# A decoder of six residual blocks on one core: golden gate weights split into four steps, constants moved, statistics between additions

## The chip, the core and the metric

One NeuronCore of a Trainium2 chip runs the whole program. TensorE (PE) multiplies matrices into eight PSUM banks of 128 x 512 floats, VectorE (DVE), ScalarE (ACT) and GpSimd (POOL) do the elementwise work, and SyncE (SP) issues most transfers. Each engine has its own list of instructions, carried out strictly in that order, and waits on semaphores for the others. The metric is the device time of one execution in microseconds (us), the median of several.

## The reference

The input x has 4 sequences of 256 tokens of 256 numbers, so 1024 tokens. Six blocks follow, each of the form "add, then normalize over the 256 numbers":

```
x = layernorm(x + linear_attention(x))            # 16 heads, elu + 1
x = layernorm(x + expert_by_token_id(x))          # 4 experts, one for each token
x = layernorm(x + golden_experts(x))              # 8 experts, all computed, weighted
x = layernorm(x + grouped_attention(x))           # groups of 32, 16 heads
x = layernorm(x + cross_attention(x, ctx, mask))
x = layernorm(x + top2_experts(x))                # 8 experts of 176, plus a shared one
```

The third is the one that the change is about. Every expert computes `(silu(x @ Wg) * (x @ Wu)) @ Wd`, and the eight results are added with weights that come from a small chain over 8 numbers per token:

```
inh      = sigmoid(x @ Wr / temperature)
in_zone  = (inh >= LOWER) & (inh <= UPPER)
distance = |inh - 1/e|
weights  = exp(-distance / 0.1) * in_zone
no_expert = sum(weights) < 1e-8
fb   = exp(-distance / 0.3), kept for the top 2 experts only, divided by its sum
weights  = fb where no_expert else weights
weights  = weights / max(sum(weights), 1e-8)
```

All results are float32. A float32 product is made of three products of rounded parts (high x high, high x low, low x high), so each operand is split into a rounded "high" part and the "low" rest.

## The kernel before, in words

The tokens are 8 tiles of 128. They are worked on in two halves, 4 tiles (512 tokens) each. Block 3, the golden experts, is done for the first half with the 8 experts and then for the second half again; it is software-pipelined with the blocks before and behind it. Its parts have these names in the program and below:

- Slot s (0 to 67) is one chunk of 128 hidden units of an expert, for 512 tokens. Expert unit u has slots 2u and 2u+1. Slots 8 to 23 are the golden experts for the first half, 24 to 39 for the second. Here m8 means step m of slot 8.
- **g** and **u** (TensorE): the gate and the up product of a slot, 6 matmuls each with 512 columns (L548, L549, L551), into banks 0 to 3. A gate product waits for the silu of the slot before the last, an up product for the hidden product (m) of two slots before.
- **s** (ScalarE L1233): silu of the gate. **m** (VectorE L1888): silu x up into `hraw`. **h** (ScalarE L1247): the high part of it. **l** (GpSimd L1489): the low part, `h_lo = hraw - h_hi`.
- **d** (TensorE L877 to L879): the down product of one expert unit, 24 matmuls of 256 columns, into banks 4 and 5, a pair of tiles in each. It waits for l of both slots of the unit, and, before it overwrites a bank, for the addition of the unit before.
- **a** (VectorE L1902): `x_tok += bank * weight`, 4 tiles, in two pairs. So a10 adds unit 10, and d11 can start only when the first pair of a10 is done.
- **G** and **D**: split of the weights of a unit into high (ScalarE L1265, L1276) and low (GpSimd L1495, L1500).
- **r0.n** and **r1.n**: the golden router for the first and the second half. r.3 is logits and sigmoid, r.4 the distance on VectorE (L1953, L1954) and its two exponentials on ScalarE (L1302, L1303), r.5 the whole chain of golden weights on VectorE (L1921 to L1940): two operations for the zone mask, three for the near weights, max and max_index for the top 2 with four behind them, and 13 more, nearly each waiting for the one before on a semaphore.
- **e0.10**, **e1.10** (VectorE L1626 to L1632): the statistics of the norm behind the golden block, for example 0 and 1 of the half (an example is one sequence of 256 tokens, two tiles); **e2.10**, **e3.10** for the second half. **c** (VectorE L1766 to L1770): constants for the later cross attention. **k4** (L1731 to L1735): which expert owns which block of the token-routed experts. **x1.50** to **x1.53** (L1761, L1763): additions and statistics for the second half of block 2.

The order of steps on each engine is written out by hand, in five lists of names (SP_ORDER, PE_ORDER, ACT_ORDER, POOL_ORDER, DVE_ORDER); the lists of PE, POOL and SP are the same before and after. The piece of PE's list that matters below is

```
g11 d4 u11 g12 u12 g13 u13 g14 u14 d5 g15 u15 d6 ...
g21 d9 u21 g22 u22 g23 u23 d10 d11 g24 u24 g25 u25 g26 e0.12 e1.12 u26 g27 u27 a0.3 d12 a0.4
```

Of the kernel before, what the change touches and what calls it, by code (L numbers as in the profile page):

```python
# [19 lines left out]
HT = TILES // 2  # L20
# [162 lines left out]
a4 m11 x1.51 m12 x1.52 x1.53 r1.0 m13 m14 a5 a6 m15 m16 m17 r1.2 a7 r1.3 a8 m18 r1.4 m19 m20 a9 m21 m22 m23 a10 a11
e0.10 e1.10 m24 r1.5 m25 e0.12 e1.12 m26 c a0.3 a12 a0.4 m27 a0.5 a0.6 m28 a0.7 m29 a0.8 a13 m30 a0.9 a0.10 a14 m31
a0.25 m32 m33 a0.11 e0.0 a15 a0.26 e1.0 m34 a16 e0.2 e1.2 m35 e0.3 e1.3 m36 e0.4 e1.4 m37 e0.5 e1.5 m38 a17 m39 e0.7
e1.7 a18 a0.22 a19 e2.10 e3.10 a0.23 m40 e2.12 e3.12 a1.3 a1.4 m41 m42 a1.5 a1.6 a1.7 a1.8 o43 m43 a1.9 o44 m44 a1.10
a1.25 o45 m45 o46 m46 a1.11 o47 m47 a1.26 e2.0 e3.0 o48 m48 e2.2 e3.2 e2.3 e3.3 o49 m49 o50 m50 e2.4 e3.4 e2.5 e3.5
o51 m51 o52 m52 e2.7 e3.7 o53 m53 a1.22 a1.23 m54 x0 m55 m56 o57 m57 o58 y0 m58 o59 m59 o60 m60 o61 m61 o62 m62 o63
m63 o64 m64 o65 m65 o66 m66 o67 m67 w0 w1 z1
""".split()  # L190


def decoder_program(nc, x_rows, x_cols, ids, pad_mask, w_attn0, w_attn1, bias_cols, bias_rows, bias_v1, bias_o,
                    w_route, temperature, consts, pk_x0, pk_f0, pk_x1, pk_f1, cw_dram, xs_dram, ys_dram, out):
    with ExitStack() as ctx:
# [103 lines left out]
        sems = {}  # L299
# [1296 lines left out]
        def _(dve):  # L1596
            links = [0]

            def link(ins):

                links[0] += 1
                ins.then_inc(sems["dve_link"], 1)
                dve.wait_ge(sems["dve_link"], links[0])
# [283 lines left out]
                    dve.wait_ge(sems["m1_done"], routed_no(u - U_F1) + 1)  # L1887
                TT(hraw[:, r, :], other[:, :], sil[:, r, :], ALU.mult).then_inc(sems["hid_mul"], 1)  # L1888

            def add(u):  # L1890

                if u < U_F0:
                    weights, e, h = route0, u, 0
                else:
                    weights, e, h = gold, (u - U_F0) % E0, (u - U_F0) // E0
                if e:
                    dve.wait_ge(sems["acc_done"], 4 * u)
                for t in range(HT):
# [15 lines left out]
                    TS(lg[:, t0:t0 + HT, :], lg[:, t0:t0 + HT, :], scale_ap, None, ALU.mult  # L1914
                       ).then_inc(sems["rt_lg"], 1)

            def gold_weights(h):

                q = slice(HT * h, HT * (h + 1))
                dve.wait_ge(sems["rt_dist"], h + 1)  # L1920
                link(TS(zone[:, q, :], inh[:, q, :], float(GOLD_LO), None, ALU.is_ge))  # L1921
                link(STT(pick[:, q, :], inh[:, q, :], float(GOLD_HI), zone[:, q, :], ALU.is_le, ALU.mult))
                dve.wait_ge(sems["rt_exp"], h + 1)
                link(TT(wz[:, q, :], wz[:, q, :], pick[:, q, :], ALU.mult))
                total(s1[:, q], wz[:, q, :])
# [12 lines left out]
                link(TS(s1[:, q], s1[:, q], 1e-8, None, ALU.max))
                link(dve.reciprocal(s2[:, q], s1[:, q]))
                link(TT(gold[:, q, :], wz[:, q, :], per_token(s2[:, q]), ALU.mult))  # L1940

            def golden(i, h):
                q = slice(HT * h, HT * (h + 1))
                if i == 0:
                    norm_stats(2 + h, begun=True)
                elif i == 2:
                    xT_low(2 + h)
                elif i == 3:
                    logits(h, temp[:, 1:2])
# [297 lines left out]
```

## Time and profile before

| | |
|---|---|
| timed runs (3) | median 431.03 us, 430.78 to 431.78 |
| the profiled execution | 432.45 us, of which the span of the trace is 430.4 |
| mean granted TensorE clock of it | 0.992 |
| TensorE (PE) busy | 409.0 us, 95% |
| VectorE (DVE) busy | 257.2 us, 60% |
| ScalarE (ACT) busy | 239.6 us, 56% |
| GpSimd (POOL) busy | 271.3 us, 63% |

The span is the time from the first to the last instruction in the trace; 2.05 us of the profiled execution lie around it. Times in rows are from the start of the span. A timeline row is: start, duration, engine, line of the kernel, operation, output <- input with partitions x elements, count of merged instructions, and in brackets how long the engine was idle before it and what released it. Instructions in a pipelined engine overlap a little, so starts and durations don't add up exactly.

### The profile page before, as it was taken

To read this page: it belongs to the slowest core of one execution; us is meant where nothing else is said; L and a number is where in the kernel's file an instruction comes from. 1 tells how busy PE (TensorE), PEld (TensorE's weight loads), DVE (VectorE), ACT (ScalarE), POOL (GpSimd) and SP (SyncE) were. 2 spreads that over 40 slices of the span, in tenths; PEclk is the share of its full clock that TensorE was granted. 3 is DMA by queue.
4 is the path that set the end of the run, shared out by engine and by line. 5 is a ranking of instruction groups with operands and counts; after the bars stand their busy time and mean duration, and the time that the engine had idled before them with its cause. 6 is when DMAs were issued, how large, how long until landed. Compare 5 with 4: busy or idle time off the path is not lost.

```text
span 430.4 us, 9389 instructions
## 1 busy us (share of the span) xinstructions
PE 409.0 (95%) x3615; PEld 354.7 (82%) x3615; DVE 257.2 (60%) x652; ACT 239.6 (56%) x429; POOL 271.3 (63%) x251
## 2 busy tenths in 40 slices
PE   8999999995999999899989999999989999999994
PEld 6888979884889888788878899798768989888983
DVE  5868757529836348966644587656445676363243
ACT  4846664673384775352733757672635757544543
POOL 2744484374598577575867548457757386877763
PEclk9999999999999999999999999999999999999998
DMA  7843022413023313042232102222532332554412
GB/s 248 288 143 116 36 68 80 148 51 122 0 79 124 105 61 124 24 126 96 76 89 76 38 0 84 68 98 62 145 116 75 115 104 79 155 161 151 140 31 99
DMA packets 22855, 43.09 MB, mean 100 GB/s; under 512 B 3051, under 2 KB 10347, under 8 KB 22812
## 3 DMA queue, kind: packets, MB, share of 16 engines
q1 hardware_dynamic: 21708, 40.92, 30.2%
q0 software_dynamic: 384, 1.05, 0.7%
q8 instruction: 29, 0.48, 0.5%
q10 hardware_dynamic: 720, 0.53, 0.4%
q14 instruction: 14, 0.11, 0.1%
HBM read 38.52 MB, written 3.44 MB: 97 GB/s over the span
## 4 chain that ended last, share of the span: by engine, by line
PE 71%; DVE 14%; ACT 5%; issue 4%; POOL 2%; DMA 2%; SPq 0%; DVEq 0%; POOLq 0%; ACTq 0%
PE bank L548 12%; PE bank L549 11%; PE bank L551 11%; PE bank L877 6%; PE bank L879 6%; PE bank L878 6%; PE bank L957 3%; DVE hraw L1888 2%; PE bank L896 2%; PE bank L945 1%; DMA q_buf<-x_cols_dram 1%; DVE x_tok L1902 1%; POOL rstd L1419 1%; PE bank L571 1%; PE bank L927 1%
## 5 line engine op out<-in xcount | busy, mean ns | idle before, releaser
L1489 POOL TENSOR_TENSOR h_lo<-hraw,h_hi 128x512 fp32r<-128x512 f32 x68 | 87.7, 1293 | 65.7 <-ACT h_hi L1247 65.5
L548 PE MATMUL bank<-xT_hi,pk_hi 128*128 128x512 f32 x240 | 97.8, 408 | 6.3 <-DVE hraw L1888 6.3
L549 PE MATMUL bank<-xT_hi,pk_lo 128*128 128x512 f32 x240 | 95.2, 397 | 0.6 <-issue 0.6
L1247 ACT ACTIVATE h_hi<-hraw 128x512 fp32r<-128x512 f32 x68 | 42.8, 629 | 75.3 <-DVE hraw L1888 75.2
L551 PE MATMUL bank<-xT_lo,pk_hi 128*128 128x512 f32 x240 | 76.0, 398 | 0.0
L1495 POOL TENSOR_TENSOR pk_lo<-pk_raw,pk_hi 128x512 fp32r<-128x512 f32 (+1 forms) x44 | 74.6, 1695 | 1.5 <-ACT pk_hi L1265 1.3
L1888 DVE TENSOR_TENSOR hraw<-bank,sil 128x512 f32<-128x512 f32 x68 | 46.9, 689 | 47.1 <-ACT sil L1233 22.6
L877 PE MATMUL bank<-pk_hi,h_hi 128*128 128x256 f32 x240 | 68.9, 287 | 0.2
L879 PE MATMUL bank<-pk_hi,h_lo 128*128 128x256 f32 x240 | 67.8, 283 | 0.0
L878 PE MATMUL bank<-pk_lo,h_hi 128*128 128x256 f32 x240 | 67.8, 282 | 0.0
L548 PEld LDWEIGHTS bank<-xT_hi,pk_hi 128*128 128x128 f32 x240 | 45.6, 190 | 17.2 <-DVE hraw L1888 7.2
L1500 POOL TENSOR_TENSOR pk_lo<-pk_raw,pk_hi 128x256 fp32r<-128x256 f32 (+1 forms) x44 | 41.9, 952 | 20.5 <-ACT pk_hi L1276 20.5
L551 PEld LDWEIGHTS bank<-xT_lo,pk_hi 128*128 128x128 f32 x240 | 45.4, 189 | 11.1 <-DVE xT_lo L1650 0.3
L549 PEld LDWEIGHTS bank<-xT_hi,pk_lo 128*128 128x128 f32 x240 | 45.7, 190 | 9.6 <-issue 0.9
L877 PEld LDWEIGHTS bank<-pk_hi,h_hi 128*128 128x128 f32 x240 | 45.8, 191 | 1.8 <-issue 0.9
L878 PEld LDWEIGHTS bank<-pk_lo,h_hi 128*128 128x128 f32 x240 | 45.8, 191 | 0.8
L879 PEld LDWEIGHTS bank<-pk_hi,h_lo 128*128 128x128 f32 x240 | 45.8, 191 | 0.0
L1276 ACT ACTIVATE pk_hi<-pk_raw 128x256 fp32r<-128x256 f32 (+1 forms) x44 | 21.5, 489 | 32.4 <-PE bank L879 32.3
L1265 ACT ACTIVATE pk_hi<-pk_raw 128x512 fp32r<-128x512 f32 (+1 forms) x44 | 34.2, 777 | 8.5 <-DMA pk_raw<-pk_f_dram 4.8
L1419 POOL TENSOR_TENSOR rstd<-var_e,mhalf 128x2 f32<-128x2 f32 (+1 forms) x19 | 15.3, 806 | 30.9 <-DVE var_e L1619 22.1
L1902 DVE SCALAR_TENSOR_TENSOR x_tok<-bank,gold,x_tok 128x256 f32<-128x256 f32 x64 | 27.2, 476 | 10.3 <-PE bank L879 10.2
L1233 ACT ACTIVATE sil<-bank 128x512 f32<-128x512 f32 x46 | 27.0, 587 | 6.1 <-PE bank L551 6.0
(306 smaller groups left out, 808.6 us busy)
## 6 DMA issues: line engine op xcount, KB each, us to landing
pk_raw<-pk_f_dram SPq DMA_DIRECT2D x28, 384.0 KB, 3.1
pk_raw<-pk_f_dram SPq DMA_DIRECT2D x16, 512.0 KB, 3.6
pk_raw<-pk_f_dram SPq DMA_DIRECT2D x16, 256.0 KB, 3.3
kv_buf<-pk_x_dram SPq DMA_DIRECT2D x4, 512.0 KB, 3.6
x_tok<-x_rows_dram SPq DMA_DIRECT2D x1, 1024.0 KB, 9.4
pk_raw<-pk_x_dram SPq DMA_DIRECT2D x4, 256.0 KB, 5.8
brow<-cw_dram SPq DMA_DIRECT2D x4, 256.0 KB, 3.2
cw_late<-cw_dram SPq DMA_DIRECT2D x4, 256.0 KB, 3.4
```

Source lines behind the costliest of these rows:

```text
L548: pe.matmul(o, w(kc)[0], x(kc)[0], start=kc == 0, stop=False)
L549: pe.matmul(o, w(kc)[1], x(kc)[0], start=False, stop=False)
L551: m = pe.matmul(o, w(kc)[0], x(kc)[1], start=False, stop=kc == KC - 1)
L877: pe.matmul(o, hh, vh, start=first, stop=False, skip_group_check=True)
L878: pe.matmul(o, hh, vl, start=False, stop=False, skip_group_check=True)
L879: m_ = pe.matmul(o, hl, vh, start=False, stop=closed and t % 2 == 1 and kc == chunks - 1, skip_group_check=True)
L1247: A(h_hi[:, row, at * 512:(at + 1) * 512], hraw[:, s % 2, :], ACT.Copy).then_inc(sems["hid_hi"], 1)
L1265: A(g_part(kind, i, pk_hi), raw, ACT.Copy).then_inc(sems["g_hi"], 1)
L1489: pool.tensor_tensor(h_lo[:, row, q], hraw[:, s % 2, :], h_hi[:, row, q].bitcast(F32), ALU.subtract).then_inc(sems["hid_lo"], 1)
L1495: pool.tensor_tensor(g_part(kind, i, pk_lo)[:, 0:w], raw_g(kind, i)[0][:, 0:w], g_part(kind, i, pk_hi)[:, 0:w].bitcast(F32), ALU.subtract) ...
L1500: pool.tensor_tensor(d_part(kind, i, pk_lo), raw_d(kind, i)[0], d_part(kind, i, pk_hi).bitcast(F32), ALU.subtract).then_inc(sems["d_lo"], 1)
L1888: TT(hraw[:, r, :], other[:, :], sil[:, r, :], ALU.mult).then_inc(sems["hid_mul"], 1)
```

## The change

Three lists of steps and two functions change.

1. The golden weights (r.5) are cut in four: the zone mask right behind the distance (in r.4), then the sum of the near weights and the top 2 (r.5), the fallback weights (r.6), and the final weights (r.7). The first half's pieces stand behind m9, m10 and m11, with x1.50 and x1.51 between, and the first golden addition (a4) goes from before m11 to behind m13. The second half's pieces go from between m24 and m25 to behind m21, m22 and m23, ahead of a10.
2. On ScalarE the two exponentials of the first half stand right behind the sigmoid, ahead of h8, instead of behind G2. One load of an activation table falls away.
3. The constants c go from before a0.3 to behind m18, k4 from before a0 to behind m5.
4. The additions a11 and a19 are cut in two pairs (A and B), with the statistics of the first example between, and m25 goes ahead of the low parts e0.12 and e1.12.

```diff
-x1.31 ... r0.2 x1.36 s8 r0.3 h8 s9 h9 G2 r0.4 s10
+x1.31 ... r0.2 x1.36 s8 r0.3 r0.4 h8 s9 h9 G2 s10
 DVE_ORDER = """
...
-k3 m1 n1.0 m2 m3 k4 a0 m4 m5 m6 a1 m7 a2 ...
+k3 m1 n1.0 m2 m3 a0 m4 m5 k4 m6 a1 m7 a2 ...
...
             elif i == 4:
...
                         ).then_inc(sems["rt_dist"], 1)
+                    gold_zone(h)
                 elif i == 5:
-                    gold_weights(h)
+                    gold_near(h)
+                elif i == 6:
+                    gold_fallback(h)
+                elif i == 7:
+                    gold_total(h)
...
-            def add(u):
+            def add(u, tiles=range(HT)):
...
                 if e:
-                    dve.wait_ge(sems["acc_done"], 4 * u)
-                for t in range(HT):
+                    dve.wait_ge(sems["acc_done"], 4 * u + tiles[0])
+                for t in tiles:
...
+                elif step[0] in "AB":
+                    add(i, range(2) if step[0] == "A" else range(2, HT))
```

The steps of VectorE in the first golden half, as the lists have them, before and after: `m9 (r0.5 whole) m10 x1.50 a4 m11 x1.51 m12 x1.52 x1.53 r1.0 m13 m14`, and `m9 r0.5 m10 x1.50 r0.6 m11 x1.51 r0.7 m12 x1.52 x1.53 r1.0 m13 a4 m14`.

The first place is VectorE at the end of the first golden half. Before, from the additions to the second of the two hidden products around the golden weights (the x2 is m19 and m20, the x3 is m21 to m23, the x8 is a10 and a11):

```order
162 L1888 TENSOR_TENSOR hraw<-bank,sil 128x512 x2
163 L1902 SCALAR_TENSOR_TENSOR x_tok<-bank,gold,x_tok 128x256 x4
164 L1888 TENSOR_TENSOR hraw<-bank,sil 128x512 x3
165 L1902 SCALAR_TENSOR_TENSOR x_tok<-bank,gold,x_tok 128x256 x8
166 L1626 BN_STATS stats<-x_tok 128x6 x2
167 L1629 BN_AGGR mv<-stats 128x2 x2
```

Now, from m22 to the statistics (the x6 is a10 and the first pair of a11):

```order
182 L1888 TENSOR_TENSOR hraw<-bank,sil 128x512
183 L1936 TENSOR_TENSOR fb<-fb,pick 128x32
184 L1670 TENSOR_REDUCE s<-fb 128x4
185 L1938 TENSOR_SCALAR s<-s 128x4
186 L1939 RECIPROCAL s<-s 128x4
187 L1940 TENSOR_TENSOR fb<-fb,s 128x32
188 L1941 TENSOR_TENSOR fb<-fb,none_in 128x32
189 L1888 TENSOR_TENSOR hraw<-bank,sil 128x512
...
196 L1952 TENSOR_TENSOR gold<-wz,s 128x32
197 L1902 SCALAR_TENSOR_TENSOR x_tok<-bank,gold,x_tok 128x256 x6
198 L1626 BN_STATS stats<-x_tok 128x6 x2
```

The golden weights of the second half now stand between m21 and a10: the near weights and the top 2 in the first piece (order rows 173 to 181, not shown), 6 between m22 and m23, and 7 between m23 and a10.

The second place is VectorE around m18 and m19. Before, m18 was followed by the distance alone, and then by m19:

```order
160 L1953 TENSOR_SCALAR zone<-inh 128x32
161 L1954 SCALAR_TENSOR_TENSOR dist<-inh,zone 128x32
```

Now the constants stand there too, and the zone mask:

```order
161 L1888 TENSOR_TENSOR hraw<-bank,sil 128x512
162 L1766 CAST cap<-mask_w 128x1024
163 L1767 TENSOR_REDUCE valid<-cap 128x4
164 L1769 TENSOR_SCALAR cap<-cap 128x1024
165 L1770 TENSOR_SCALAR bk_four<-con,bcol 128x4
166 L1965 TENSOR_SCALAR zone<-inh 128x32
167 L1966 SCALAR_TENSOR_TENSOR dist<-inh,zone 128x32
168 L1921 TENSOR_SCALAR zone<-inh 128x32
169 L1922 SCALAR_TENSOR_TENSOR pick<-inh,zone 128x32
170 L1888 TENSOR_TENSOR hraw<-bank,sil 128x512 x2
```

So eight operations stand between m18 and m19 (the first of the x2), where there were two.

## Rows read from the trace of the kernel before

**Rows 1.** TensorE's waits over the whole span: engine, operation, releaser, total us, times, longest.

```profile
PE bank L548 <- DVE hraw L1888: 6.7, 3, 5.2
```

**Rows 2.** Stretch 100 to 120 us: length, busy by engine, clock, DMA.

```profile
100.00:120.00 20.00, 14.83 (x70) 12.19 (x69) 16.37 (x42) 7.41 (x13) 10.53 (x10) 0.91 0.13 44
```

**Rows 3.** Timeline of TensorE, g12's end, u12's start, d5's start.

```profile
100.54 0.63 PE L551 MATMUL bank<-xT_lo,pk_hi 128*128 128x512 f32 x2
106.33 0.80 PE L548 MATMUL bank<-xT_hi,pk_hi 128*128 128x512 f32 x1 [5.17 <-DVE hraw L1888]
...
114.86 0.28 PE L877 MATMUL bank<-pk_hi,h_hi 128*128 128x256 f32 x1
```

**Rows 4.** Timeline of VectorE, first half's golden weights: m9, two stalled steps, x1.53.

```profile
92.27 0.69 DVE L1888 TENSOR_TENSOR hraw<-bank,sil 128x512 f32<-128x512 f32 x1 [2.71 <-ACT sil L1233]
...
96.34 1.07 DVE L1924 TENSOR_TENSOR wz<-wz,pick 128x32 f32<-128x32 f32 x1 [3.07 <-ACT fb L1303]
...
101.27 2.10 DVE L1930 TENSOR_SCALAR s<-s 128x4 f32<-128x4 f32 x1
...
112.23 1.49 DVE L1761 TENSOR_TENSOR x_tok<-x_tok,o_tok 128x256 f32<-128x256 f32 x1
```

**Rows 5.** Timeline of GpSimd beside them: low part of G3, l12.

```profile
101.00 2.34 POOL L1495 TENSOR_TENSOR pk_lo<-pk_raw,pk_hi 128x1024 fp32r<-128x1024 f32 x1 [0.48 <-ACT pk_hi L1265]
...
112.15 1.29 POOL L1489 TENSOR_TENSOR h_lo<-hraw,h_hi 128x512 fp32r<-128x512 f32 x1 [0.74 <-ACT h_hi L1247]
```

**Rows 6.** Timeline of ScalarE, the first half's exponential.

```profile
95.89 0.23 ACT L1302 ACTIVATE wz<-dist 128x32 f32<-128x32 f32 x1
```

**Rows 7.** Timeline of VectorE, second half's stretch: m19, m21, a10, a stalled golden step.

```profile
143.84 0.69 DVE L1888 TENSOR_TENSOR hraw<-bank,sil 128x512 f32<-128x512 f32 x1 [2.20 <-ACT sil L1233]
...
153.47 0.69 DVE L1888 TENSOR_TENSOR hraw<-bank,sil 128x512 f32<-128x512 f32 x1 [2.33 <-ACT sil L1233]
...
158.77 0.88 DVE L1902 SCALAR_TENSOR_TENSOR x_tok<-bank,gold,x_tok 128x256 f32<-128x256 f32 x2 [0.72 <-PE bank L879]
...
168.77 1.27 DVE L1926 TENSOR_SCALAR none_in<-s 128x4 f32<-128x4 f32 x1
```

**Rows 8.** Busy time of VectorE: golden weights (first), m21's end to a10 (second).

```profile
167.85:174.80 6.95, 6.16 (x36) 1.00 0.13 52
...
154.10:158.80 4.70, 1.48 (x4) 1.00 0.08 31
```

**Rows 9.** Busy time in the constants' stretch, of instructions on `cap` alone.

```profile
177.30:182.40 5.10, 2.60 (x3) 1.00 0.18 51
```

**Rows 10.** Timeline of GpSimd: l19, l21, l23, low part of G8.

```profile
145.27 1.29 POOL L1489 TENSOR_TENSOR h_lo<-hraw,h_hi 128x512 fp32r<-128x512 f32 x1 [2.06 <-ACT h_hi L1247]
...
154.91 1.30 POOL L1489 TENSOR_TENSOR h_lo<-hraw,h_hi 128x512 fp32r<-128x512 f32 x1 [1.34 <-ACT h_hi L1247]
...
158.79 1.29 POOL L1489 TENSOR_TENSOR h_lo<-hraw,h_hi 128x512 fp32r<-128x512 f32 x1 [0.65 <-ACT h_hi L1247]
160.04 2.41 POOL L1495 TENSOR_TENSOR pk_lo<-pk_raw,pk_hi 128x1024 fp32r<-128x1024 f32 x1
```

**Rows 11.** Timeline of TensorE: d9, d11, u27, a0.4.

```profile
147.19 0.28 PE L877 MATMUL bank<-pk_hi,h_hi 128*128 128x256 f32 x1
...
160.18 0.36 PE L877 MATMUL bank<-pk_hi,h_hi 128*128 128x256 f32 x1
...
175.51 0.50 PE L548 MATMUL bank<-xT_hi,pk_hi 128*128 128x512 f32 x1 [1.15 <-DVE hraw L1888]
...
183.01 0.51 PE L548 MATMUL bank<-xT_hi,wa_hi 128*128 128x512 f32 x1 [0.16 <-DVE q_buf L1962]
```

**Rows 12.** Timeline of VectorE, the hidden product m4.

```profile
55.54 0.69 DVE L1888 TENSOR_TENSOR hraw<-bank,sil 128x512 f32<-128x512 f32 x1
```

**Rows 13.** Timeline of ScalarE, the silu of slot 4.

```profile
54.86 0.58 ACT L1233 ACTIVATE sil<-bank 128x512 f32<-128x512 f32 x1
```

**Rows 14.** Timeline of GpSimd, a low part at the end of the second golden half.

```profile
267.54 1.32 POOL L1495 TENSOR_TENSOR pk_lo<-pk_raw,pk_hi 128x512 fp32r<-128x512 f32 x1
```

More of the change, by code:

```diff
@@ L158 @@
 s4 h4 s5 h5 G1 s6 h6 D1 s7 h7 x1.00 x1.01 x1.10 x1.02 x1.11 x1.20 x1.03 x1.12 x1.21 x1.04 x1.30 x1.13 x1.22 x1.05
-x1.31 x1.14 x1.23 x1.06 x1.32 x1.15 x1.24 x1.33 x1.16 x1.25 x1.34 x1.26 x1.35 r0.2 x1.36 s8 r0.3 h8 s9 h9 G2 r0.4 s10
+x1.31 x1.14 x1.23 x1.06 x1.32 x1.15 x1.24 x1.33 x1.16 x1.25 x1.34 x1.26 x1.35 r0.2 x1.36 s8 r0.3 r0.4 h8 s9 h9 G2 s10
 D2 G3 h10 s11 h11 s12 h12 s13 h13 s14 D3 G4 r1.1 h14 s15 S0 D4 G5 h15 s16 h16 s17 r1.2 h17 D5 G6 D6 s18 r1.3 h18 s19
@@ L180 @@
 k0 p2 b0.0 b0.1 b0.2 b0.3 b0.4 b0.5 k1 b1.0 b0.6 b0.7 b1.1 b0.8 p5 b1.2 n0.0 b1.3 b1.4 b1.5 b1.6 b1.7 n0.2 b1.8 k2 m0
-k3 m1 n1.0 m2 m3 k4 a0 m4 m5 m6 a1 m7 a2 x1.00 x1.01 a3 x1.10 x1.02 x1.11 x1.20 x1.03 x1.40 x1.12 x1.21 x1.04 x1.41
+k3 m1 n1.0 m2 m3 a0 m4 m5 k4 m6 a1 m7 a2 x1.00 x1.01 a3 x1.10 x1.02 x1.11 x1.20 x1.03 x1.40 x1.12 x1.21 x1.04 x1.41
 x1.13 x1.22 x1.05 x1.42 x1.14 x1.23 x1.06 x1.43 r0.0 x1.15 x1.24 x1.16 x1.25 x1.26 r0.2 r0.3 m8 r0.4 m9 r0.5 m10 x1.50
[L183 to L189, printed above, removed]
+r0.6 m11 x1.51 r0.7 m12 x1.52 x1.53 r1.0 m13 a4 m14 a5 a6 m15 m16 m17 r1.2 a7 r1.3 a8 m18 c r1.4 m19 m20 a9 m21 r1.5
+m22 r1.6 m23 r1.7 a10 A11 e0.10 B11 e1.10 m24 m25 e0.12 e1.12 m26 a0.3 a12 a0.4 m27 a0.5 a0.6 m28 a0.7 m29 a0.8 a13
+m30 a0.9 a0.10 a14 m31 a0.25 m32 m33 a0.11 e0.0 a15 a0.26 e1.0 m34 a16 e0.2 e1.2 m35 e0.3 e1.3 m36 e0.4 e1.4 m37 e0.5
+e1.5 m38 a17 m39 e0.7 e1.7 a18 a0.22 A19 e2.10 B19 e3.10 m40 a0.23 e2.12 e3.12 a1.3 a1.4 m41 m42 a1.5 a1.6 a1.7 a1.8
+o43 m43 a1.9 o44 m44 a1.10 a1.25 o45 m45 o46 m46 a1.11 o47 m47 a1.26 e2.0 e3.0 o48 m48 e2.2 e3.2 e2.3 e3.3 o49 m49 o50
+m50 e2.4 e3.4 e2.5 e3.5 o51 m51 o52 m52 e2.7 e3.7 o53 m53 a1.22 a1.23 m54 x0 m55 m56 o57 m57 o58 y0 m58 o59 m59 o60
+m60 o61 m61 o62 m62 o63 m63 o64 m64 o65 m65 o66 m66 o67 m67 w0 w1 z1
 """.split()
@@ L1915, in logits, with gold_zone @@
                        ).then_inc(sems["rt_lg"], 1)
-            def gold_weights(h):
+            def gold_zone(h):
                 q = slice(HT * h, HT * (h + 1))
@@ L1922, in gold_weights, with gold_near @@
                 link(STT(pick[:, q, :], inh[:, q, :], float(GOLD_HI), zone[:, q, :], ALU.is_le, ALU.mult))
+            def gold_near(h):
+                q = slice(HT * h, HT * (h + 1))
                 dve.wait_ge(sems["rt_exp"], h + 1)
@@ L1927, in gold_weights, with gold_fallback @@
                 top2(fb, h)
+            def gold_fallback(h):
+                q = slice(HT * h, HT * (h + 1))
                 link(TT(fb[:, q, :], fb[:, q, :], pick[:, q, :], ALU.mult))
@@ L1933, in gold_weights, with gold_total @@
                 link(TT(fb[:, q, :], fb[:, q, :], per_token(none_in[:, q]), ALU.mult))
+            def gold_total(h):
+                q = slice(HT * h, HT * (h + 1))
                 link(TS(s2[:, q], none_in[:, q], -1.0, 1.0, ALU.mult, ALU.add))
```

## The prediction

> **What bounds the kernel now.** I read the list of TensorE's waits first, then the stretches of the span by engine, then the timelines of TensorE, VectorE and GpSimd side by side in the stretches where the edits stand. TensorE is nearly always busy, so a change of order can only win what TensorE waits for, and it loses whatever new wait it makes. The reader is to see in the list that TensorE waits for the hidden products for 6.7 us in three places, one of them 5.2 us long [rows 1]. That one is u12, which starts at 106.33 because it needs m10, and m10 stands behind the whole chain of golden weights of the first half [rows 3]. The stretch around it is also the only one in the middle of the span with a granted clock under 1 [rows 2]. The second wait is u27's, 1.15 us, behind the same chain of the second half, and a0.4 waits 0.16 us behind the constants [rows 11].
>
> In VectorE's timeline the chain's small steps take about 0.2 us, but some take 1 to 2 us: 1.07 at 96.34, 2.10 at 101.27, 1.49 at 112.23, 1.27 at 168.77 [rows 4, 7]. The step at 101.27 ends at 103.37, and GpSimd's subtraction that began at 101.00 ends at 103.34. The one at 112.23 ends 0.3 us after GpSimd's l12 at 113.44 [rows 4, 5]. So a step of the chain that meets a running GpSimd subtraction stands until that is over. This decides the case, since the edit puts the pieces behind hidden products, and 0.75 us after each hidden product's end GpSimd starts its l: m21 ends at 154.16, l21 starts at 154.91 and runs to 156.21 [rows 7, 10].
>
> The Trainium skill, "SBUF — State Buffer", section "SBUF: two separate sides", says that VectorE and GpSimd share a pair of ports, held by one instruction from start to end, and that VectorE needs it for two SBUF inputs or a two-port mode. The trace agrees by the 2.10 us step. By that rule the locks are structural and the pieces pay them anew wherever they are put; without it the long steps would be accidents, which is the rival "no stalls" below.
>
> **The sum, part by part.** Steps are dated in the clock of the profiled execution; its 432.45 us is 1.42 above the median of the three runs, and the span of 430.4 has 2.05 around it.
>
> k4 (four tiny operations) leaves the place before a0. m4 starts at 55.54, but its silu ends at 54.86 + 0.58 = 55.44 [rows 12, 13], so m4 can't go earlier than it does. Behind m5 it has an idle VectorE. 0, with 0.6 at most if it is held by an l there.
>
> First half. The exponentials move ahead, from 95.89 [rows 6] to about 89.6, right behind the distance; they hold h8 back 0.7 us and through it m9 by 0.35 us (92.27 becomes 92.6) and d4 by 0.2. The chain on VectorE then starts behind m9, at 93.2 instead of 96.34 [rows 4]: 3.1 us earlier. What stands between there and d5 is now: the chain without its zone mask (5.35 us, worked out below), m10 to m13 (4 x 0.6), x1.50 to x1.53 with their statistics (4 x 0.86 and 0.65), and the first pair of a4 (0.88), in all 12.7 us. Laid beside GpSimd's list, l9, the low parts of G2, D2 and G3, l10, l11 and l12 each catch one step: 0.2 + 2.1 + 0.9 + 1.95 + 0.85 + 1.1 + 1.1 = 8.2 us, and 0.3 for the late restart that x1.53 shows. So a4's first pair is done at 93.2 + 12.7 + 8.2 + 0.3 = 114.4, and d5, which needs it because a4 now stands behind m13, starts at about 114.5. Before it started at 114.86 [rows 3]. u12's wait of 5.17 us is gone, but u13 (1.6), u14 (1.3) and d5 (3.4) wait in its place. -0.3 us. The bounds: without any stall d5 would start when TensorE is ready, 5.17 + 1.5 = 6.7 us earlier (1.5 being the slow clock behind the wait; rows 2 give 0.09 x 20 = 1.8 at most); with one more subtraction met, 1.3 later.
>
> Constants behind m18. The three operations on the mask are 2.60 us [rows 9], bk_four 0.17, the two of the zone mask 0.4, so 3.2 us more between m18 and m19, where VectorE idled 2.20 [rows 7]. m19 is 1.1 us late, l19 too: it ended at 146.56, 0.55 before d9 needed it at 147.19 [rows 10, 11]. d9 is 0.55 late. The bounds are 0.3 and 1.8 (l18 caught too).
>
> Golden weights ahead of a10. In the stretch from 167.85 the chain took 6.9 us [rows 8], less 1.1 for the stall at 168.77, less 0.4 for the mask: 5.35 us of work, by its number of steps 2.4, 1.35 and 1.55 for the three pieces. VectorE idled 4.70 - 1.48 = 3.2 us between m21 and a10 [rows 8]. With no stall a10 would be 2.1 late; its first pair had 0.5 us to spare against d11 (158.77 + 0.88 to 160.18 [rows 7, 11]), so d11 would be 1.6 late. With stalls: the first piece is caught by l21 at its cast and ends 156.8 (0.25 of stall), m22 ends 157.5. l22 starts 158.25; the second piece has done four of its six steps by then, the fifth stands to 159.6 (1.05), m23 is at 159.8 instead of 157.36 and ends 160.5. l23 runs 161.26 to 162.56; the third piece has seven steps, the fifth stands until 162.6 (1.05), and the seventh then meets the low part of G8, 2.41 us long, which follows l23 at once [rows 10], until 164.95 (1.95). a10 starts at 164.9, its first pair ends 165.8, and d11 starts at 165.9 instead of 160.18: +5.7. If the seventh step slips in ahead of G8, it is +3.2.
>
> What comes back. From d11 on m24 and m25 need no golden weights: u27's 1.15, a0.4's 0.16 and the slow first matmul after each (0.2) go [rows 11]. -1.5. The split a11 costs nothing, since its statistics fill the time in which VectorE waited for the second pair.
>
> The split a19. The first statistics come 1.3 us earlier, the second 0.55, but their small steps now fall at 267.5, where a GpSimd subtraction starts at 267.54 and runs 1.32 [rows 14]. -0.25 if they pass, +0.7 if caught. I take 0.
>
> Clock. d11 waits longer than u12 did, and behind u12's wait matmuls ran at the lower level, 1.2 GHz instead of 2.4 (a mean of 0.91 over 20 us). The price is 0 to 1.8 [rows 2]; the median lies 1.4 under the profiled execution, so I read a slow stretch as something that most executions were spared, and take 0.3. The Trainium skill, "TensorE: Matmul & The Clock Gate", section "HAM oscillation — how this bites in real kernels", has waits that put TensorE back to the half clock; by it alone the term would be nearer its upper end.
>
> Sum: 0 - 0.3 + 0.55 + 5.7 - 1.5 + 0 + 0.3 = +4.75, so 432.45 + 4.75 = 437.2 us. Taken from the median, which seems to lack the slow stretch: there the first half is 1.2 dearer instead of 0.3 cheaper, 431.03 + 1.2 + 0.55 + 5.7 - 1.5 + 0.3 = 437.3, the same.
>
> **Rivals.**
>
> One: the third piece slips in ahead of G8's low part. For it: a waiting step was let in between two GpSimd operations in the trace. Against: the last step is issued only 0.2 us after the fifth is let in, when G8 is already running. 437.2 - 2.5 = 434.7.
>
> Two, the other side: no stalls. The pieces would fit the gaps of GpSimd, and u12's wait goes for good: first half -6.7, constants +0.3, d11 +1.6, back -1.5: 432.45 - 6.3 = 426.2. The place is the first half, the price the 8.2 us of stalls there. With half the stalls in both halves it is 432.45 - 4.4 + 0.45 + 3.7 - 1.5 = 430.7, so it is faster only when more than half of them are missing. For it: this chain is long only where GpSimd works, and small shifts move the meetings. Against: l comes 0.75 us behind each m by construction, so each piece longer than that is caught.
>
> Three: the halves cancel. d11 late by 1.6 to 3.2, the first half better by 2 to 3: about 431.
>
> **How the numbers follow.** The forecast, 437.2 with its own range 435.5 to 438.8, gets 0.62; rival one 0.20; rival two 0.08, and rival three 0.10, of which half is within 0.2% and the rest divided between the sides. A difference of 0.2% (0.86 us) is about what a measurement of this kernel can tell from no change. Slower: 0.62 + 0.20 + 0.03 = 0.85. Same: 0.05. Faster: 0.10. The range that leaves out about 2 in 10 is 432.4 to 438.8.
>
> **What would show each step.** Right: u12 starts at about 101.2 with no wait, d5 waits some 3 us for VectorE (L1902) and starts near 114.5; d9 has a short wait for GpSimd; TensorE is idle some 5 us ahead of d11, released by L1902, with a golden TENSOR_TENSOR of about 2 us in VectorE's timeline just before; no wait at u27. Wrong: d11 waits under 2 us, or the steps of the three pieces all take 0.2 us; then the stalls were mis-sized, and the forecast with them. If d5 starts at 108 to 111 the first half was.

## The result, and the profile after

The changed kernel takes 440.38 us (median of four runs, 437.94 to 440.70) against 430.9 for the kernel before (four runs, 430.7 to 431.78): a ratio of 1.0204, 95% interval 1.0164 to 1.0243. In a second comparison, beside other kernels (the run after_again below), it was 1.0191 (1.0163 to 1.0218). It is slower, as forecast, but by 9 us and not by 6: the forecast was 437.2, and its range ended at 438.8. The profiled execution took 440.55 us, its span is 438.6.

TensorE's waits over the whole span (operation, releaser, total us, times, longest); the one row of [rows 1] is now the second here:

```profile
PE bank L877 <- DVE x_tok L1902: 9.1, 2, 5.9
PE bank L548 <- DVE hraw L1888: 3.0, 3, 1.5
PE bank L957 <- issue: 2.0, 3, 1.2
PE bank L571 <- ACT x_tok L1120: 1.6, 2, 1.3
```

The 5.2 us in front of a hidden product are gone. Two waits for the additions have come, 3.3 and 5.9 us. The granted clock of two stretches (the columns are those of [rows 2]):

```profile
100.00:120.00 20.00, 14.20 (x60) 11.58 (x59) 15.96 (x36) 5.22 (x11) 8.70 (x7) 0.83 0.12 39
160.00:180.00 20.00, 14.13 (x72) 12.72 (x71) 13.57 (x36) 6.56 (x12) 11.77 (x11) 0.83 0.22 66
```

[Rows 2] had 0.91 in the first, and the second was at 1.00 in the trace of before. The timeline of TensorE shows whom that hit: d5, g15, d9 and d11, the answers to [rows 3, 11].

```profile
113.84 0.55 PE L877 MATMUL bank<-pk_hi,h_hi 128*128 128x256 f32 x1 [3.27 <-DVE x_tok L1902]
...
119.10 0.63 PE L548 MATMUL bank<-xT_hi,pk_hi 128*128 128x512 f32 x1
...
149.55 0.36 PE L877 MATMUL bank<-pk_hi,h_hi 128*128 128x256 f32 x1 [0.43 <-issue]
...
168.40 0.55 PE L877 MATMUL bank<-pk_hi,h_hi 128*128 128x256 f32 x1 [5.87 <-DVE x_tok L1902]
168.75 0.41 PE L878 MATMUL bank<-pk_lo,h_hi 128*128 128x256 f32 x1
168.96 0.41 PE L879 MATMUL bank<-pk_hi,h_lo 128*128 128x256 f32 x1
```

A down product is 24 such matmuls. d5 takes from 113.84 to 119.10, 5.26 us, where d5 of before took from 114.86 to 117.73, 2.87. Rows of d11 stand 0.21 us apart, where a down product elsewhere has a step of 0.12 (2.87 / 24). Both ran at the lower of the two clock levels, 1.2 GHz instead of 2.4: the granted clock is 0.83 in either stretch of 20 us, 1.00 in those between.

VectorE in the first half (m9, five golden steps, x1.53, a4), and GpSimd beside it, to be laid next to [rows 4, 5]:

```profile
91.60 0.69 DVE L1888 TENSOR_TENSOR hraw<-bank,sil 128x512 f32<-128x512 f32 x1 [2.58 <-ACT sil L1233]
...
94.40 2.33 DVE L1665 TENSOR_TENSOR zone<-con,top_f 128x32 f32<-128x32 f32 x1
...
98.61 1.24 DVE L1936 TENSOR_TENSOR fb<-fb,pick 128x32 f32<-128x32 f32 x1
...
100.52 2.27 DVE L1940 TENSOR_TENSOR fb<-fb,s 128x32 f32<-128x32 f32 x1
102.83 1.20 DVE L1941 TENSOR_TENSOR fb<-fb,none_in 128x32 f32<-128x32 f32 x1
...
105.58 1.24 DVE L1946 TENSOR_SCALAR s<-none_in 128x4 f32<-128x4 f32 x1
...
109.69 1.48 DVE L1761 TENSOR_TENSOR x_tok<-x_tok,o_tok 128x256 f32<-128x256 f32 x1
...
112.83 1.65 DVE L1902 SCALAR_TENSOR_TENSOR x_tok<-bank,gold,x_tok 128x256 f32<-128x256 f32 x4
```

```profile
94.29 2.39 POOL L1495 TENSOR_TENSOR pk_lo<-pk_raw,pk_hi 128x1024 fp32r<-128x1024 f32 x1
...
98.51 1.29 POOL L1500 TENSOR_TENSOR pk_lo<-pk_raw,pk_hi 128x512 fp32r<-128x512 f32 x1 [1.83 <-ACT pk_hi L1276]
100.34 2.40 POOL L1495 TENSOR_TENSOR pk_lo<-pk_raw,pk_hi 128x1024 fp32r<-128x1024 f32 x1 [0.54 <-ACT pk_hi L1265]
102.70 1.28 POOL L1489 TENSOR_TENSOR h_lo<-hraw,h_hi 128x512 fp32r<-128x512 f32 x1
```

Each long golden step of VectorE shown beside its subtraction ends with it, 0.05 us behind: 94.40 + 2.33 = 96.73 and 94.29 + 2.39 = 96.68; 99.85 and 99.80; 102.79 and 102.74; 104.03 and 103.98. The second half looks the same, m21, three long steps (and a RECIPROCAL that isn't long) and a10, and l21, l23 and the low part of G8, next to [rows 7, 10]:

```profile
155.90 0.69 DVE L1888 TENSOR_TENSOR hraw<-bank,sil 128x512 f32<-128x512 f32 x1 [2.34 <-ACT sil L1233]
...
160.71 1.32 DVE L1940 TENSOR_TENSOR fb<-fb,s 128x32 f32<-128x32 f32 x1
...
163.77 1.25 DVE L1950 TENSOR_SCALAR s<-s 128x4 f32<-128x4 f32 x1
165.06 0.18 DVE L1951 RECIPROCAL s<-s 128x4 f32<-128x4 f32 x1
165.27 2.07 DVE L1952 TENSOR_TENSOR gold<-wz,s 128x32 f32<-128x32 f32 x1
167.38 1.66 DVE L1902 SCALAR_TENSOR_TENSOR x_tok<-bank,gold,x_tok 128x256 f32<-128x256 f32 x4
```

```profile
157.34 1.29 POOL L1489 TENSOR_TENSOR h_lo<-hraw,h_hi 128x512 fp32r<-128x512 f32 x1 [1.35 <-ACT h_hi L1247]
...
163.73 1.27 POOL L1489 TENSOR_TENSOR h_lo<-hraw,h_hi 128x512 fp32r<-128x512 f32 x1 [1.74 <-ACT h_hi L1247]
164.95 2.34 POOL L1495 TENSOR_TENSOR pk_lo<-pk_raw,pk_hi 128x1024 fp32r<-128x1024 f32 x1
```

TensorE's program has the same order in both kernels, so the starts of its down products can be subtracted pair by pair. The trace of after runs 0.98 us ahead before the change begins (0.52 of it is a wait of TensorE at the very start of the kernel in the trace of before), so 0.98 is added to its times:

| point | before | after + 0.98 | late by | of that, new | forecast |
|---|---|---|---|---|---|
| d5 starts | 114.86 | 114.82 | 0.0 | 0.0 | -0.3 |
| d6 starts | 120.52 | 123.25 | 2.7 | +2.7, clock at d5 | in the clock's 0.3 |
| d9 starts | 147.19 | 150.53 | 3.3 | +0.6, constants | +0.55 |
| d11 starts | 160.18 | 169.38 | 9.2 | +5.9, golden weights | +5.7 |
| d12 starts | 179.82 | 189.86 | 10.0 | +2.7 clock at d11, -1.9 back | -1.5 back |
| e2.12 starts | 270.96 | 279.18 | 8.2 | -1.8, waits named issue and small | 0 |
| e3.12 and d20 on | 283.00 | 292.01 | 9.0 | +0.8, a19 | 0 |
| last matmul | 423.81 | 432.95 | 9.1 | +0.1 | 0 |

The 2.7 at d11 is the 5.26 us of d11 less 2.95, and 0.4 for the end of the slow stretch under g24, as at d5. The -1.8 is mostly one wait of 1.19 us, named issue, ahead of line 957 at 219.31 in the trace of before; after has none there, the second profiled execution of after one of 0.90, so it goes with the execution and not with the change.

### The profile page after: what moved, and what is told of

Its sections match the earlier page's. It is cut to its first block, busy times and chain, and to the rows that moved or that the text cites. A ratio compares the mean times of both kernels' runs of the same rounds, so it can differ in the third digit from the quotient of the medians.

```text
span 438.6 us, 9391 instructions
## 1 busy us (share of the span) xinstructions
PE 412.4 (94%) x3615; PEld 358.9 (82%) x3615; DVE 262.6 (60%) x652; ACT 238.3 (54%) x428; POOL 270.7 (62%) x251
## 3 DMA queue, kind: packets, MB, share of 16 engines
q0 software_dynamic: 384, 1.05, 0.7%
## 4 chain that ended last, share of the span: by engine, by line
PE 72%; DVE 13%; ACT 5%; issue 4%; POOL 4%; DMA 0%; SPq 0%; DVEq 0%; POOLq 0%; ACTq 0%
PE bank L548 11%; PE bank L549 11%; PE bank L551 10%; PE bank L877 7%; PE bank L879 6%; PE bank L878 6%; PE bank L957 2%; DVE hraw L1888 2%; PE bank L896 2%; PE bank L945 1%; PE bank L571 1%; ACT L1233 1%; POOL rstd L1419 1%; PE bank L735 1%; POOL xs_dram L1440 1%
## 5 line engine op out<-in xcount | busy, mean ns | idle before, releaser
L877 PE MATMUL bank<-pk_hi,h_hi 128*128 128x256 f32 x240 | 71.3, 297 | 9.9 <-DVE x_tok L1902 9.1
L879 PE MATMUL bank<-pk_hi,h_lo 128*128 128x256 f32 x240 | 69.9, 291 | 0.0
L878 PE MATMUL bank<-pk_lo,h_hi 128*128 128x256 f32 x240 | 69.9, 291 | 0.0
L877 PEld LDWEIGHTS bank<-pk_hi,h_hi 128*128 128x128 f32 x240 | 47.9, 200 | 12.3 <-issue 11.5
L878 PEld LDWEIGHTS bank<-pk_lo,h_hi 128*128 128x128 f32 x240 | 48.1, 200 | 0.7
L879 PEld LDWEIGHTS bank<-pk_hi,h_lo 128*128 128x128 f32 x240 | 48.0, 200 | 0.0
```

Source lines behind the costliest of these rows:

```text
L877: pe.matmul(o, hh, vh, start=first, stop=False, skip_group_check=True)
L878: pe.matmul(o, hh, vl, start=False, stop=False, skip_group_check=True)
L879: m_ = pe.matmul(o, hl, vh, start=False, stop=closed and t % 2 == 1 and kc == chunks - 1, skip_group_check=True)
```

## The experiments

Ratios are to the kernel before, run on the same chip within the same set.

**fill.** Before the steps d5 and d11 TensorE gets products that nobody reads.

```diff
+            def fill(s, n):
+                pe.wait_ge(sems["silu_done"], s - 1)
+                for j in range(n):
+                    pe.matmul(bank[2 * (s % 2)][:, :], x_tile(xT_hi, j % KC, 0), x_half(xT_hi, j % KC, 0),
+                              start=True, stop=True)
+FILLS = {"d5": (15, 15), "d11": (24, 26)}
```

> The changed kernel, but TensorE gets products that nobody reads while it waits: 15 of 512 columns (into the bank of g15, before g15) ahead of d5, and 26 (into the bank of g24, before g24) ahead of d11. Theory (the wait for VectorE puts the clock down, and d5 and d11 pay for it): both waits stay in time but are filled, d5 and d11 take about 2.95 us each instead of 5.26, the two long stretches at the lower clock are gone, and the time falls by 4.6 us to about 435.8. Rival (the lower clock at d5 and d11 comes from something else than the idle engine, or costs nothing because what follows waits anyway): 440.4, within 0.5.

Measured: 435.66 us, 1.0088 (1.0057 to 1.0118), so about 1.0% or 4.4 us under the changed kernel's 1.0191 and 5.0 under its 1.0204. The timeline of TensorE: fillers, d5, g15, and the fillers of d11.

```profile
110.54 3.67 PE L1087 MATMUL bank<-xT_hi 128*128 128x512 f32 x15
114.04 0.28 PE L878 MATMUL bank<-pk_hi,h_hi 128*128 128x256 f32 x1
...
116.91 0.40 PE L549 MATMUL bank<-xT_hi,pk_hi 128*128 128x512 f32 x1
...
159.80 6.23 PE L1087 MATMUL bank<-xT_hi 128*128 128x512 f32 x26
```

d5 starts 0.2 us later than in the changed kernel and ends 2.2 us earlier: 2.87 us instead of 5.26. (The line numbers of this kernel are 1 higher on TensorE and 10 higher on VectorE.) VectorE's lateness is untouched. The uncertainty of either difference is about 1.8 us, so the rival (no gain) is out and the 4.6 of the theory fits: the low clock behind the two waits is worth 4.4 to 5 us.

**second_back.** The second half's pieces go back between m24 and m25.

```diff
-... a9 m21 r1.5 m22 r1.6 m23 r1.7 a10 A11 e0.10 B11 e1.10 m24 m25 e0.12
+... a9 m21 m22 m23 a10 A11 e0.10 B11 e1.10 m24 r1.5 r1.6 r1.7 m25 e0.12
```

> The changed kernel with the three pieces of the second half's golden weights put back between m24 and m25. Theory (the wait ahead of d11 cost 5.7 and its slow clock 2.3, and 1.3 came back at u27 and a0.4): 440.4 - 8.0 + 1.3 = 433.7. Rival, by the terms of the prediction alone, in which the clock is worth 0.3: 440.4 - 5.7 + 1.5 - 0.3 = 435.9. d11 starts some 6 us earlier with no wait, and u27 waits about 1.2 us again.

Measured: 433.31 us, 1.0029 (1.0000 to 1.0057), 7.0 us under the changed kernel by these ratios, with an uncertainty of 1.7. The theory had 6.7, the sum with a clock of 0.3 had 4.5, which is out. The wait ahead of d11 is gone. u27 doesn't wait either, but it is still held by VectorE's chain: m25 (the first row, VectorE) ends at 174.81, and u27 (the second, TensorE) starts right behind it.

```profile
174.12 0.69 DVE L1888 TENSOR_TENSOR hraw<-bank,sil 128x512 f32<-128x512 f32 x1
```

```profile
174.87 0.50 PE L548 MATMUL bank<-xT_hi,pk_hi 128*128 128x512 f32 x1
```

This trace runs 0.90 us ahead of the one of before, so u27 starts 0.26 later than before, not earlier; TensorE merely got there later (d11 is 0.7 late behind the constants, and a transposed example takes longer). By d12, 0.4 us have come back here, where 1.9 come back in the changed kernel. So 1.5 of the 1.9 belong to the moved pieces. The chain between m24 and m25, which takes 6.95 us in the kernel before with a step of 1.27 in it [rows 7, 8], takes 5.6 here (168.55 to 174.12) and meets GpSimd for 0.2 only.

The wait ahead of d5 is as long as in the changed kernel, but in this profiled execution no slow stretch follows it, and nine of the twelve executions have a clock of 0.993 to 0.998, three of 0.987 to 0.990.

**a19_back.**

```diff
-e1.7 a18 a0.22 A19 e2.10 B19 e3.10 m40 a0.23
+e1.7 a18 a0.22 a19 e2.10 e3.10 a0.23 m40
```

> The changed kernel with the last golden expert's additions of the second half whole again and their statistics behind them, as before. Theory read from the profile after (the small steps of the first statistics are caught by a GpSimd subtraction, and TensorE waits 1.28 us for the transposed example instead of 0.37): 0.9 us faster, 439.5. Rival, the value of the prediction: no difference, 440.4.

Measured: 438.97 us, 1.0164 (1.0124 to 1.0204), 1.2 us under 1.0191 with an uncertainty of 2 us; the time can't tell 0.9 from 0. The profiles can. In the changed kernel VectorE's small step meets the low part on GpSimd, and ScalarE's rows for e3.12 are late (one row each of VectorE, GpSimd and TensorE):

```profile
274.81 1.32 DVE L1631 TENSOR_SCALAR minus_mean<-mv 128x2 f32<-128x2 f32 x1
```

```profile
274.78 1.32 POOL L1495 TENSOR_TENSOR pk_lo<-pk_raw,pk_hi 128x512 fp32r<-128x512 f32 x1
```

```profile
280.15 0.84 PE L571 MATMUL bank<-con,x_tok 128*128 128x128 f32 x4 [1.28 <-ACT x_tok L1120]
```

With a19 whole the same step takes 0.17 us and TensorE waits 0.37:

```profile
276.62 0.17 DVE L1631 TENSOR_SCALAR minus_mean<-mv 128x2 f32<-128x2 f32 x1
```

```profile
279.90 0.84 PE L571 MATMUL bank<-con,x_tok 128*128 128x128 f32 x4 [0.37 <-ACT x_tok L1120]
```

**short_lows.** GpSimd's subtractions beside the two places, shortened.

```diff
+                if s in (9, 10, 11, 12, 21, 22, 23):
+                    q = slice(at * 512, at * 512 + 64)
+                if kind == "f0" and i in (2, 3, 8):
+                    w = 128
+                w = 64 if kind == "f0" and i == 2 else d_part(kind, i, pk_lo).shape[1]
```

> The changed kernel with part of GpSimd's work left out: the low parts of the hidden products of slots 9 to 12 and 21 to 23 are computed for 64 of 512 columns, those of the golden weights G2, G3 and G8 for 128 of 1024, of D2 for 64 of 512. Theory (small steps of VectorE stand until a running GpSimd subtraction ends, 8.2 us of it in the first half and 4.3 in the second, and TensorE's clock pays for the waits): the waits at u13, u14 and d5 (1.5, 1.0, 3.3) go, d11 waits 1.6 instead of 5.9, and both slow stretches go or shrink: 440.4 - 5.8 - 4.1 - 4.6 = about 426. Rival (the steps are long for another reason, such as their own operands or the queue): the same waits, 440.4, at most 1 less.

Measured: 427.43 us, 0.9903 (0.9865 to 0.9941), 12 to 13 us under the changed kernel with the same order of work. The steps that took 1.24 and 2.27 above take the time of their neighbours, and d5 starts 4.75 us earlier (VectorE's line numbers are 5 higher here):

```profile
96.54 0.19 DVE L1941 TENSOR_TENSOR fb<-fb,pick 128x32 f32<-128x32 f32 x1
...
97.40 0.19 DVE L1945 TENSOR_TENSOR fb<-fb,s 128x32 f32<-128x32 f32 x1
```

```profile
109.09 0.36 PE L877 MATMUL bank<-pk_hi,h_hi 128*128 128x256 f32 x1 [1.80 <-DVE x_tok L1907]
```

So the steps were long because GpSimd's subtractions ran beside them; the rival, their own operands or the queue, is out, since neither changed. The expectation missed in one point: d5 still waits 1.8 us. Even without long steps, d5 is 4.75 us earlier and not the 6.7 that the prediction had for that case.

**after_again.** The changed kernel once more.

> The changed kernel once more, beside the others on one chip, so that they are compared within one set of runs. Theory (waits of VectorE and two slow stretches, the second rare in no execution): 1.020 of before, granted clocks of 0.98 to 0.991. Rival (part of the difference belonged to the chip of the first comparison): 1.014 or less, near the prediction.

Measured: 440.16 us, 1.0191 (1.0163 to 1.0218), granted clocks 0.983 to 0.990. Its profiled execution was one of the quicker ones, 437.86 us, and shows why: the stretches of TensorE as above, then d5 and g15.

```profile
100.00:120.00 20.00, 14.20 (x73) 11.27 (x72) 16.05 (x35) 7.59 (x15) 11.11 (x9) 1.00 0.13 41
160.00:180.00 20.00, 14.48 (x69) 12.80 (x70) 12.67 (x34) 8.32 (x16) 10.47 (x10) 0.83 0.20 66
```

```profile
113.68 0.36 PE L877 MATMUL bank<-pk_hi,h_hi 128*128 128x256 f32 x1 [3.26 <-DVE x_tok L1902]
...
116.62 0.40 PE L548 MATMUL bank<-xT_hi,pk_hi 128*128 128x512 f32 x1
```

Same kernel, same wait of 3.26 us, full clock behind it: d5 takes 2.94 us, and the span is 435.9 instead of 438.6. That is 2.7 us for one slow stretch. Of the ten executions of the changed kernel three have a mean clock of 0.989 to 0.991 and take 437.9 to 438.3 us, seven have 0.983 to 0.987 and take 440.1 to 441.0. So the wait of 3.3 us was followed by the lower clock in about seven of ten; in second_back, which has the same wait, the clocks say three of twelve, so the share is not fixed. The two groups lie as far apart as one slow stretch is worth. All ten clocks are below the 0.993 to 0.997 of a kernel whose wait is filled (fill_before2 below), so it is likely, though not shown for each, that all have the stretch behind the 5.9 us wait.

**first_back.** The first half as before: exponentials behind G2, the pieces together between m9 and m10, a4 ahead of m11.

```diff
-r0.5 m10 x1.50 r0.6 m11 x1.51 r0.7 m12 x1.52 x1.53 r1.0 m13 a4 m14
+r0.5 r0.6 r0.7 m10 x1.50 a4 m11 x1.51 m12 x1.52 x1.53 r1.0 m13 m14
```

> The changed kernel with the first half as before: the exponentials behind G2, the golden weights in one piece between m9 and m10, a4 ahead of m11. Theory (the waits of the first half are as long after as before, but d5 runs at the lower clock behind its wait; g15 starts 2.3 us later after than before, dated from the same point): about 2.3 faster than the changed kernel, 1.0150 of before instead of 1.0204. Rival, the prediction's term: 0.3 slower, 1.021.

Measured: 438.2 us, 1.0150 (1.0113 to 1.0186), 1.8 us under 1.0191 and 2.3 under 1.0204, each with an uncertainty of about 2, so the time alone fits the theory (1.0150) without proving it. d5 starts at 113.74 here and at 113.84 in the changed kernel, so the VectorE work was moved for nothing. But this kernel has its slow stretch as well, behind u12's wait of 4.76 us, and has paid for it when d5 starts; the stretch reads:

```profile
100.00:120.00 20.00, 15.38 (x71) 12.99 (x72) 14.92 (x37) 7.59 (x14) 10.81 (x9) 0.83 0.15 41
```

The changed kernel pays behind the start of d5, on top, in the executions that have the stretch there. Equal starts of d5 are not equal outcomes.

**fill_before** and **fill_before2.** Fillers in the kernel before, where u12 waits.

```diff
+FILLS = {"u12": (13, 22)}    # fill_before
+FILLS = {"g12": (12, 20)}    # fill_before2
```

> The kernel before, but TensorE gets 22 products of 512 columns that nobody reads (into the bank of g13, before g13) while u12 waits 5.2 us for m10. Theory (every execution of before pays for the lower clock behind this wait, as the clocks of 0.987 to 0.993 in all its runs suggest): 1.5 faster, 0.9965 of before. Rival, the prediction's reading (the profiled execution alone had the slow stretch): no difference within 0.3 us, 1.000.

Measured: 436.71 us, 1.0109 (1.0076 to 1.0143): slower, and no test of either theory. The fillers wait for the silu of slot 11, which ScalarE issues behind h10, which needs m10, for which u12 waits too. They start when the wait is over and push u12 back by their whole length:

```profile
107.04 7.62 PE L1087 MATMUL bank<-xT_hi 128*128 128x512 f32 x22 [6.31 <-ACT sil L1243]
```

> The kernel before, with 20 products of 512 columns that nobody reads ahead of g12 (into its own bank), in the place where TensorE would have waited for u12: 4.7 us of filling for 5.2 us of waiting, and they need only the silu of slot 10, so they don't start late. Theory (every execution of before pays for the lower clock behind u12's wait): 1.5 faster, 0.9965 of before. Rival, the prediction's reading (the profiled execution alone had the slow stretch): no difference within 0.3 us, 1.000.

Measured: 428.01 us, 0.9937 (0.9911 to 0.9964). The fillers, u12, and the stretch's clock:

```profile
98.74 4.83 PE L1087 MATMUL bank<-xT_hi 128*128 128x512 f32 x20
...
105.53 0.50 PE L549 MATMUL bank<-xT_hi,pk_hi 128*128 128x512 f32 x1 [0.56 <-DVE hraw L1898]
```

```profile
100.00:120.00 20.00, 19.42 (x100) 15.89 (x99) 15.65 (x40) 8.48 (x16) 12.01 (x9) 1.00 0.17 49
```

The kernel before gains 2.7 us (1.6 to 3.8) from 20 products that nobody reads. Its own executions have clocks of 0.983 to 0.995 in all sets, around 0.989, and those of this version 0.993 to 0.997. So the lower clock behind u12's wait is paid in most executions of before. The profiled one, with 0.992, was a mild case: from the start of u12 to the start of d5 it took 8.53 us (106.33 to 114.86), first_back with its longer stretch 9.13 (104.61 to 113.74), and this kernel 7.39 (105.53 to 112.92). A stretch behind u12 so cost 1.1 and 1.7 us in the two profiles that have one; what the 2.7 holds beyond that is within its uncertainty.

**gates_first**, **gates_first_c**, **g4_ahead**, **m13_ahead.** Versions meant to be faster.

```diff
# gates_first, from the changed kernel: second_back and a19_back, and
-PE: g14 u14 d5 g15 u15 d6            ACT: s14 D3 G4 r1.1 h14 s15 S0
+PE: g14 u14 g15 u15 d5 d6            ACT: s14 D3 G4 r1.1 s15 h14 S0
# gates_first_c, from gates_first: DVE m18 r1.4 ... e1.12 m26 c a0.3
# g4_ahead, from gates_first: ACT s14 G4 D3, POOL l13 G4 D3 l14
# m13_ahead, from g4_ahead: DVE x1.52 m13 x1.53 r1.0 a4
```

> A version meant to be faster: the changed kernel with the second half's pieces put back between m24 and m25, the additions a19 whole again, and g15 and u15 ahead of d5 on TensorE (with the silu of slot 15 ahead of h14 on ScalarE), so that the wait for a4 is spent on products that need only m13. Theory: from 433.3 of the kernel with the second half put back, 2.3 to 2.8 of the 3.3 us wait are filled, 0.9 comes back with a19, and no slow stretch is left at d5: 429.5, or 0.994 of before. Rival (h14 waits for d5, so l14, l15 and d6 or d7 come late by what was won): 433, or 1.002 of before.

> The same with the constants put back behind m26. Theory (behind m18 they make d9 0.4 to 0.55 late, and behind m26 they hold a0.4 up by 0.2): 0.3 us faster than with the constants behind m18, so 429.2, with no wait of TensorE at d9 and a short one at a0.4. Rival (behind m26 they cost what they did before the change, 1.3 at u27 and a0.4 together): 0.8 slower, 430.3.

Measured: 430.94 us, 0.9959 (0.9938 to 0.9980), and 430.42, 0.9964 (0.9942 to 0.9986). The wait for a4 is spent on g15 and u15, and both versions beat the kernel before. Where the constants stand makes no difference that this comparison can tell. 0.994 was expected of gates_first, just inside its interval. One wait is new in the timeline of TensorE: g16 waits for the low part of G4, which stands behind D3, which waits for the end of d5.

```profile
121.97 0.50 PE L548 MATMUL bank<-xT_hi,pk_hi 128*128 128x512 f32 x1 [1.60 <-POOL pk_lo L1495]
```

> The version with g15 and u15 ahead of d5, and the split of the golden weights G4 ahead of D3 on ScalarE and GpSimd. In that version g16 waits 1.6 us for the low part of G4, which stands behind D3, and D3 needs the end of d5. Theory: G4 needs nothing of d5, its low part is done by about 117.5 instead of 121.9, the wait goes, and the time falls from 0.9959 of before by 1.6 us to 0.992. Rival (G4's transfer isn't there that early, or its low part holds l14 or a step of VectorE up): 0.996.

> The same as g4_ahead, with m13 ahead of x1.53 and its statistics on VectorE. Theory: m13 ends at 110.4 instead of 112.9, u15 doesn't wait its 1.0 us, and a4 is no later than u15's end: 1.0 faster than g4_ahead, 0.990. Rival (l13 now meets the steps between m13 and a4, so d5 waits what u15 waited): equal to g4_ahead, 0.992.

Measured: 428.99 us, 0.9947 (0.9918 to 0.9975), and 428.17, 0.9915 (0.9889 to 0.9941). g16's wait and then u15's are gone from the profiles; the step from gates_first to g4_ahead is 0.5 us by the ratios where 1.6 was expected, within the uncertainty of both. m13_ahead has the lowest ratio, 3.7 us under the kernel before and 12 under the changed one; fill_before2 (0.9937) lies within the uncertainty of it. Its d5, now behind u15, starts without a wait:

```profile
113.30 0.36 PE L877 MATMUL bank<-pk_hi,h_hi 128*128 128x256 f32 x1
```

## Why the prediction was right in its waits and wrong in its time

**k4**, 0: right. m4 starts at 54.56, where 55.54 less the 0.98 of the earlier start puts it.

**First half**, -0.3: right as a sum of waits. u12's wait is gone, and 1.5, 1.0 and 3.27 us stand at u13, u14 and d5, as forecast (1.6, 1.3, 3.4). d5 starts 0.04 earlier. The long steps add up to 8.7 us more than their usual lengths (2.33 for 0.19, 2.27 for 0.19 and so on, seven steps), where 8.2 were forecast. The mechanism is shown by short_lows.

**Constants**, +0.55: the table has +0.6.

**Golden weights ahead of a10**, +5.7: measured +5.9. The long steps are 0.43 (the cast), 1.32, 1.25 and 2.07, of which 0.25, 1.1, 1.1 and 1.9 are stall where 0.25, 1.05, 1.05 and 1.95 were forecast, and the last step did meet the low part of G8, so rival one is out.

**What comes back**, -1.5: -1.9 by the table. Second_back, with the pieces between m24 and m25 again, still gets 0.4 of the 1.9, so the pieces account for the 1.5 that the prediction gave them. The last half of item 4 of the change has no part in it: m25 stood ahead of e0.12 and e1.12 in the list before too.

**The split a19**, 0 between -0.25 and +0.7: it was caught, +0.8, at the upper bound or just over it. In the trace of after GpSimd is at one subtraction after another from 269.65 to 276.10, and the small step at 274.81 falls into the last. The prediction had named such a subtraction [rows 14] and then took the middle; with GpSimd busy for 6.4 us on end, "caught" was the value to take. The profile of a19_back has neither the long step nor the long wait; the time can't tell.

**The clock**, +0.3: this is the step that failed. The prediction read "a slow stretch as something that most executions were spared", because the median lay 1.4 us under the profiled execution, and it bounded the price by 1.8, from the 0.91 of [rows 2]. The first is refuted and the second doesn't carry over. Taking the idle time away made the kernel before faster by 2.7 (1.6 to 3.8), so most of its executions pay. And 0.91 is the reading of one mild case at one place: the same view of after has 0.83 twice, that is 0.17 x 20 = 3.4 us of lost clock each, part of it in the wait itself, where [rows 2] gave 1.8. Behind u12 the stretch cost 1.1 and 1.7 us in the profiles, under that bound; behind d5 and d11 it cost 2.7. The sum also took the slow stretch of before out (it is in the d5 of 114.86) and put none in its place. Measured: 2.7 behind each of the two waits in the profiled execution, 5.4 in all, of which fill gives back 4.4 to 5.0 over all executions; by their clocks, three in ten pay 2.7 only.

The four profiles with a 5.9 us wait ahead of d11 (after, after_again, a19_back, first_back) all show the lower clock behind it; of the four with a 3.3 us wait ahead of d5 two do (after, a19_back) and two don't (after_again, second_back). The Trainium skill, "TensorE: Matmul & The Clock Gate", section "HAM oscillation — how this bites in real kernels", has waits that put TensorE back to the half clock; the traces agree for all 5.9 us waits and for half of the 3.3 us waits, and the prediction gave it too little weight.

The Trainium skill, "SBUF — State Buffer", section "SBUF: two separate sides", has VectorE or GpSimd blocked for as long as an instruction of the other holds the ports that they share. Short_lows agrees: steps of 1.24 and 2.27 us went to 0.19 when the subtractions were short.

With the sum's own terms and the measured clock and a19, 432.45 - 0.3 + 0.55 + 5.7 - 1.5 + 5.4 + 0.8 = 443.1; the 0.98 of the start, 1.4 of the waits named issue and 0.4 of small ones bring it to 440.3, and 440.55 was profiled.

Rival two, no stalls, is what short_lows made real: it gave 426.2, and 427.43 was measured (0.9903 of before) with the subtractions shortened beside the two places.

## What to carry to other kernels

When a change puts a wait in front of TensorE, add to its length what TensorE does right behind it at half clock: here 2.7 us behind a wait of 5.9 us each time, and behind one of 3.3 us in some executions only. If a wait can't be removed, put a product in front of it that needs none of what is waited for; even one that nobody reads can pay, provided that it doesn't wait for the same chain. Before a small step of VectorE is moved, lay the place beside GpSimd's list: a step of 0.2 us costs what is left of the subtraction it meets (not every kind of step, see below). And a wait that is gone from a trace is not yet time won: compare the starts of the same step.

## What the runs showed of the hardware that was not expected

One kernel, the changed one, waits 3.27 and 3.26 us ahead of d5 in its two profiled executions and runs at 1.2 GHz behind the first wait and at 2.4 behind the second, with 2.7 us of span between them. It has two groups of times, around 438 and 440.5, without any change in the order of its work, and the mean granted clock of an execution (0.989 to 0.991, or 0.983 to 0.987) tells them apart.

What a slow stretch costs depends on its place: 1.1 and 1.7 us behind u12, 2.7 behind d5 and d11.

On VectorE, RECIPROCAL took 0.18 us at 165.06 with GpSimd's low part of G8 running (164.95 to 167.29), and the TENSOR_TENSOR behind it 2.07: not every small step of VectorE stands behind GpSimd. Which kinds do beyond those in the rows was not tried here.
